# Row-tiled pairs for the maxima products of a two-layer attention kernel

## The reference

```python
def layer0(x, cond, attn_mask, ...):
    h = _ada_norm(x, cond, ln1_g, ln1_b, ada1_w, ada1_b)
    q, k, v = (_split_heads(h @ w + b) for w, b in ((wq, bq), (wk, bk), (wv, bv)))
    q, k = _apply_rotary(q, sin, cos), _apply_rotary(k, sin, cos)
    scores = einsum('bhqd,bhkd->bhqk', q, k) / sqrt(32)
    scores = where(attn_mask, scores, -inf)
    out = einsum('bhqk,bhkd->bhqd', softmax(scores), v)
    x = x + merge(out) @ wo + bo
    h = _ada_norm(x, cond, ln2_g, ln2_b, ada2_w, ada2_b)
    return x + gelu(h @ ff_w1 + ff_b1) @ ff_w2 + ff_b2

def layer1(x, c, ...):
    sh1, sc1, g1, sh2, sc2, g2 = split(silu(c) @ wc.T + bc, 6)
    x = x + g1 * gqa_attn(ln(x) * (1 + sc1) + sh1, wq, wk, wv, wo)   # 16 query heads, 4 key heads
    return x + g2 * (gelu((ln(x) * (1 + sc2) + sh2) @ w1.T + b1) @ w2.T + b2)
```

## Time and profile before

| what | before |
|---|---|
| median of 3 runs | 3960.23 us (3954.39 to 3964.08) |
| span of the profiled execution | 3966.3 us |
| PE busy | 3790.3 us (96%), 20404 products |
| DVE busy | 2467.7 us (62%) |
| ACT busy | 1601.7 us (40%) |
| POOL busy | 1603.3 us (40%) |
| mean granted clock of PE | 0.976 of full speed |

### The profile page before, as it was taken

How to read it: one execution, slowest core, us unless ns; L and a number is a source line. 1 busy time by engine, 2 the same in 40 slices (tenths; PEclk the granted TensorE clock), 3 DMA queues, 4 the chain that set the end, 5 groups by cost and what they waited for, 6 DMA issues and landing times.

```text
span 3966.3 us, 53519 instructions
## 1 busy us (share of the span) xinstructions
PE 3790.3 (96%) x20404; PEld 1507.3 (38%) x20404; DVE 2467.7 (62%) x3951; ACT 1601.7 (40%) x2807; POOL 1603.3 (40%) x907
## 2 busy tenths in 40 slices
PE   7988999999999999999999999999999999999999
PEld 4422444233443335432254323433244333533344
DVE  5687735766457655576654777367664776467752
ACT  1465313554125642155521663136521563126621
POOL 2466212673216632066510672136520672226611
PEclk8899999999999999999999999999999999999999
DMA  5233243212433123331233012311123112311122
GB/s 155 56 98 111 82 107 84 80 41 89 104 80 81 44 87 93 103 81 44 105 96 94 22 41 91 111 44 28 62 94 101 31 39 80 109 59 25 62 67 96
DMA packets 139021, 305.21 MB, mean 77 GB/s; under 512 B 19680, under 2 KB 59636, under 8 KB 137872
## 3 DMA queue, kind: packets, MB, share of 16 engines
q10 hardware_dynamic: 50944, 174.62, 13.6%
q1 hardware_dynamic: 87824, 127.17, 12.2%
HBM read 223.46 MB, written 36.66 MB: 66 GB/s over the span
## 4 chain that ended last, share of the span: by engine, by line
PE 83%; DVE 8%; POOL 3%; issue 3%; ACT 3%; DMA 1%; ACTq 0%; SPq 0%; POOLq 0%; DVEq 0%
PE ps L834 12%; PE ps L836 12%; PE ps L835 12%; PE ps L1014 11%; PE ps L935 9%; PE ps L997 8%; PE ps L871 7%; PE ps L1029 5%; DVE mcol L1517 3%; PE ps L888 3%; ACT probs L1194 2%; POOL sums L730 2%; DVE ring L1567 2%; PE ps L852 1%; DVE turn L1451 1%
## 5 line engine op out<-in xcount | busy, mean ns | idle before, releaser
L1517 DVE TENSOR_REDUCE mcol<-ps 128x1 f32<-128x512 f32 x2048 | 1288.5, 682 | 470.6 <-PE ps L935 470.2
L730 POOL TENSOR_TENSOR sums<-probs 128x1024 f32<-128x1024 f32 x448 | 1057.6, 2376 | 967.6 <-PE ps L1029 525.9
L1194 ACT ACTIVATE probs<-ps 128x512 f32<-128x512 f32 x2048 | 1098.2, 608 | 826.9 <-PE ps L997 592.8
L935 PE MATMUL ps<-ks,qs 97*128 97x512 f16 x2048 | 789.4, 389 | 61.3 <-DVE mcol L1517 43.6
L997 PE MATMUL ps<-qs,ks 98*128 98x512 f16 x2048 | 773.2, 387 | 72.3 <-ACT probs L1194 67.2
L1340 ACT ACTIVATE sums<-ps,cols 128x512 f32<-128x512 f32 x256 | 175.8, 687 | 1096.9 <-PE ps L836 1096.9
L1014 PE MATMUL ps<-probs,v_sb 128*32 128x512 f32 x4096 | 567.0, 628 | 0.0
L935 PEld LDWEIGHTS ps<-ks,qs 97*128 97x128 f16 x2048 | 201.2, 99 | 619.0 <-DVE mcol L1517 361.9
L834 PE MATMUL ps<-ring,probs 128*128 128x512 f16 x1024 | 388.0, 379 | 0.3 <-DVE probs L1612 0.3
L834 PE MATMUL ps<-aT,ring 128*128 128x512 f16 x1024 | 388.0, 379 | 0.0
L836 PE MATMUL ps<-aT,ring 128*128 128x512 f16 x1024 | 388.0, 379 | 0.0
(11 more groups left out here) (110 smaller groups left out, 3293.4 us busy)
## 6 DMA issues: line engine op xcount, KB each, us to landing
ring<-halves ACTq DMA_DIRECT2D x208, 512.0 KB, 3.4
qs<-hl SPq DMA_DIRECT2D x192, 128.0 KB, 4.0
ring<-halves SPq DMA_DIRECT2D x48, 512.0 KB, 6.3
ring<-in_weights ACTq DMA_DIRECT2D x39, 512.0 KB, 4.3
halves<-ring ACTq DMA_DIRECT2D x37, 512.0 KB, 2.9
ks<-hl SPq DMA_DIRECT2D x120, 128.0 KB, 4.3
dcopy<-inverses SPq DMA_DIRECT2D x56, 256.0 KB
probs<-in_x SPq DMA_DIRECT2D x8, 1024.0 KB, 8.3
```

Source lines behind the costliest of these rows:

```text
L730: pool.tensor_tensor(sums[:, m % SUM_SLOTS, :, :], prob(u - 2), prob(u), ALU.add).then_inc(sum_set[0].sem, 1)
L935: pe.matmul(bank, qs[0:K_MAX, hh, h, P * qt:P * qt + P], ks[0:K_MAX, key_set(i, hh), key_head(i, hh, h), 512 * half:512 * half + 512], sta ...
L1194: act.activation(prob(u)[:, e, :], ps[:, w % SCORE_BANKS, :], ACT.Exp).then_inc(exp_done.sem, 1)
L1517: dve.tensor_reduce(mcol[:, blk % 2, 4 * j + qt, half:half + 1], src, AX.X, ALU.max).then_inc(n_free[0], 1)
```

## The change

The stacks are laid out anew, so that the high x high rows of a head lie within the first 64 partitions for the even heads of a block and within the last 64 for the odd ones. In layer 0 the pair's rows are 0 to 32 and 64 to 96 (high part and mask row), in layer 1 0 to 63 and 64 to 96. In attention the maxima of two heads, over these rows alone, are issued as a pair (`max_pair`): two products over 33 (or 64) rows in different halves of the array, into two banks; the pair first waits for both banks. The products with low parts are thus left out of these maxima (in layer 1 the even heads keep one of the two); scores, from which they are subtracted, keep all rows. The 36 maxima outside attention stay products over 97 rows.

A step now issues one pair, then the four scores (with fills between the second and the fourth as before), then its other pairs. `MAX_AT_K` is made even, so that steps of block 1 in layer 0 have 4, 6, 4, 6, 4, 4 and 4 maxima in place of 5, 4, 5, 4, 5, 4 and 5.

SyncE's copies change with the layout: a layer 0 build is twelve DMAs of 64 partitions in place of six of 128, a layer 1 query build six in place of three, the row of maxima two in place of one, and the mask rows of layer 0 are two. The semaphore counts follow (`STACK_DONE`, `STACK_BEFORE`). The order of a block's heads in the packed weights and in the rotary table is changed to match.

```diff
@@ -25,7 +25,13 @@
-
+KEY_BASES = (((0, 65), (33,)), ((32, 64), (0,)))
+QUERY_BASES = (((0, 33), (65,)), ((0, 64), (32,)))
+PAIR_ROWS = (slice(0, HD + 1), slice(2 * HD, 3 * HD + 1))
+MASK_ROW, MAX_ROW = (HD, 3 * HD), 3 * HD + 1
+SHARED_KEY_BASES = ((0, 64), (32,))
+PLAIN_QUERY_BASES = (((0, 32), (64,)), ((32, 64), (0,)))
+PLAIN_PAIR_ROWS = (slice(0, 2 * HD), slice(2 * HD, 3 * HD + 1))
 NB = 2 * B
 UNITS, STEPS = 128, 64
...
@@ -38,7 +44,7 @@
 Q_CHUNKS = 2
 L0_CHUNKS, L1_CHUNKS = 24, 21
 MAX_AT = (4, 6, 8, 10, 12, 14, 16, 18, 20, 22, 24, 26, 28, 30, 32)
-MAX_AT_K = (0, 2, 5, 7, 9, 11, 14, 16, 18, 20, 23, 25, 27, 29, 32)
+MAX_AT_K = (0, 2, 4, 6, 10, 12, 14, 16, 20, 22, 24, 26, 28, 30, 32)
 WO_AT = 53
 LN2_AT = 60
 BIAS_AT = (49, 49, 50, 51, 53, 54, 56, 56)
...
@@ -66,7 +72,18 @@
 def max_tile(k):
-    return k // 2 % 4, k // 8, k % 2
+
+    pair, odd = divmod(k, 2)
+    return 2 * (pair // 8) + odd, pair % 8 // 2, pair % 2
+
+
+def slot_of(g, j):
+
+    return 4 * (j % 2) + 2 * g + j // 2
+
+
+def max_place(j, qt):
+    return 8 * (j % 2) + 4 * (j // 2) + qt
 def sum_of(u):
...
@@ -524,40 +540,52 @@
                 st, heads = key_set(i, hh), 8 if layer(i) == 0 else 4
                 if layer(i) == 0:
-                    m = mask_rows[i:i + 1, :].rearrange("o (h k) -> o h k", h=1).broadcast_to([1, heads, S])
+                    m = mask_rows[i:i + 1, :].rearrange("o (h k) -> o h k", h=1).broadcast_to([1, 4, S])
+                    for odd in range(2):
+                        r = MASK_ROW[odd]
+                        sp.dma_start(ks[r:r + 1, st, 4 * odd:4 * odd + 4, :], m).then_inc(mask_in[st], 16)
                 else:
                     m = ins["rows"][2:3, :].rearrange("o (h k) -> o h k", h=1).broadcast_to([1, heads, S])
-                sp.dma_start(ks[96:97, st, 0:heads, :], m).then_inc(mask_in[st], 16)
+                    sp.dma_start(ks[96:97, st, 0:heads, :], m).then_inc(mask_in[st], 16)
                 one = ins["rows"][1:2, :].rearrange("o (h k) -> o h k", h=1).broadcast_to([1, heads, S])
-                sp.dma_start(ks[97:98, st, 0:heads, :], one).then_inc(mask_in[st], 16)
+                sp.dma_start(ks[MAX_ROW:MAX_ROW + 1, st, 0:heads, :], one).then_inc(mask_in[st], 16)
             def put_stack(key):
                 kind, i, hh, th, part = key
                 done, _ = stack_done(key)
+                tok = slice(512 * th, 512 * th + 512)
                 if layer(i) == 0:
                     sp.wait_ge(st_lo, BUILDS[key] + 1)
-                    rows, heads, pieces = 16, slice(0, 8), [(0, 0), (0, 1), (1, 0), (1, 1)]
-                else:
-                    sp.wait_ge(*freed(key))
-                    sp.wait_ge(st_hi, BUILDS[key] + 1)
-                    rows, heads, pieces = 32, slice(4 * part, 4 * part + 4), [(0, BUILDS[key] % 2), (1, BUILDS[key] % 2)]
-                for low, x in pieces:
-                    src = hl[:, 2 * low + x, :]
-                    hi_at = (0, 64) if kind == "k" else (0, 32)
-                    for base in ((32 if kind == "k" else 64,) if low else hi_at):
-                        r0 = base + (16 * x if layer(i) == 0 else 0)
-                        if kind == "k":
-                            dst = ks[r0:r0 + rows, key_set(i, hh), heads, 512 * th:512 * th + 512]
-                        else:
-                            dst = qs[r0:r0 + rows, hh, heads, :]
-                        sp.dma_start(dst, src).then_inc(done, 16)
+                    for odd in range(2):
+                        half, slots = slice(64 * odd, 64 * odd + 64), slice(4 * odd, 4 * odd + 4)
+                        for low in range(2):
+                            for base in (KEY_BASES if kind == "k" else QUERY_BASES)[odd][low]:
+                                for x in range(2):
+                                    r = slice(base + ROT * x, base + ROT * x + ROT)
+                                    dst = ks[r, key_set(i, hh), slots, tok] if kind == "k" else qs[r, hh, slots, :]
+                                    sp.dma_start(dst, hl[half, 2 * low + x, :]).then_inc(done, 16)
+                    return
+                sp.wait_ge(*freed(key))
+                sp.wait_ge(st_hi, BUILDS[key] + 1)
+                for low in range(2):
+                    x = 2 * low + BUILDS[key] % 2
+                    if kind == "k":
+                        for base in SHARED_KEY_BASES[low]:
+                            sp.dma_start(ks[base:base + HD, key_set(i, hh), 0:4, tok], hl[:, x, :]).then_inc(done, 16)
+                        continue
+                    for odd in range(2):
+                        slots = slice(4 * odd + 2 * part, 4 * odd + 2 * part + 2)
+                        for base in PLAIN_QUERY_BASES[odd][low]:
+                            sp.dma_start(qs[base:base + HD, hh, slots, :], hl[64 * odd:64 * odd + 64, x, :]
+                                         ).then_inc(done, 16)
             def put_rows(i, blk):
                 hh, qc, g = block_of(blk)
                 sp.wait_ge(*freed(("rows", i, blk)))
-                d = qs[97:98, hh, 4 * g:4 * g + 4, :]
-                dst = bass.AP(d.tensor, d.offset, [[d.ap[0][0], 1], [P, 16], [1, P]])
-                sp.dma_start(dst, mT[:, :]).then_inc(max_in.sem, 16)
+                for odd in range(2):
+                    d = qs[MAX_ROW:MAX_ROW + 1, hh, 4 * odd + 2 * g:4 * odd + 2 * g + 2, :]
+                    dst = bass.AP(d.tensor, d.offset, [[d.ap[0][0], 1], [P, 8], [1, P]])
+                    sp.dma_start(dst, mT[8 * odd:8 * odd + 8, :]).then_inc(max_in.sem, 16)
             def totals_out(i, blk):
...
@@ -924,17 +954,32 @@
                                            start=(c == 0), stop=(c == C - 1))
                 mm.then_inc(n_full, 1)
+            def max_operands(key):
+                _, i, blk, k = key
+                hh, qc, g = block_of(blk)
+                j, qt, half = max_tile(k)
+                query = qs[:, hh, slot_of(g, j), P * qt:P * qt + P]
+                keys = ks[:, key_set(i, hh), key_slot(i, hh, g, j), 512 * half:512 * half + 512]
+                return j, query, keys
+
             def max_item(key):
                 _, i, blk, k = key
-                hh, qc, g = block_of(blk)
                 if k == 0:
                     stacks_ready(i, blk)
                 bank = bank_free(key)
-                j, qt, half = max_tile(k)
-                h = 4 * g + j
-                pe.matmul(bank, qs[0:K_MAX, hh, h, P * qt:P * qt + P],
-                          ks[0:K_MAX, key_set(i, hh), key_head(i, hh, h), 512 * half:512 * half + 512],
-                          start=True, stop=True).then_inc(n_full, 1)
+                _, query, keys = max_operands(key)
+                pe.matmul(bank, query[0:K_MAX], keys[0:K_MAX], start=True, stop=True).then_inc(n_full, 1)
+
+            def max_pair(two):
+
+                _, i, blk, k = two[0]
+                if k == 0:
+                    stacks_ready(i, blk)
+                banks = [bank_free(key) for key in two]
+                for bank, key in zip(banks, two):
+                    j, query, keys = max_operands(key)
+                    rows = (PAIR_ROWS if layer(i) == 0 else PLAIN_PAIR_ROWS)[j % 2]
+                    pe.matmul(bank, query[rows], keys[rows], start=True, stop=True).then_inc(n_full, 1)
             def stacks_ready(i, blk):
                 hh, qc, g = block_of(blk)
...
@@ -987,15 +1032,15 @@
             def score(i, w):
                 hh, qc, g = block_of(w // 32)
-                kt, h, bank = w % 32 // 4, 4 * g + w % 4, w % SCORE_BANKS
+                kt, j, bank = w % 32 // 4, w % 4, w % SCORE_BANKS
                 if w % 32 == 0:
                     pe.wait_ge(max_in.sem, max_in.at(i, w // 32 + 1))
                 if w >= SCORE_BANKS:
                     pe.wait_ge(exp_done.sem, exp_done.at(i, w - SCORE_BANKS + 1))
                 elif i >= 1:
                     pe.wait_ge(y_read.sem, y_read.at(i - 1, 5 + bank))
-                pe.matmul(ps[:, bank, :], ks[0:K_EXP, key_set(i, hh), key_head(i, hh, h), P * kt:P * kt + P],
-                          qs[0:K_EXP, hh, h, :], start=True, stop=True).then_inc(s_mm.sem, 1)
+                pe.matmul(ps[:, bank, :], ks[0:K_EXP, key_set(i, hh), key_slot(i, hh, g, j), P * kt:P * kt + P],
+                          qs[0:K_EXP, hh, slot_of(g, j), :], start=True, stop=True).then_inc(s_mm.sem, 1)
             def values(i, u):
                 hh, qc, g = block_of(u // 16)
...
@@ -1035,20 +1080,20 @@
                     u = 2 * s
                     if s < STEPS:
                         maxima, fills = maxima_at(i, s), FILLS[i].get(s, [])
-                        some(maxima[0:1])
+                        pairs = [maxima[n:n + 2] for n in range(0, len(maxima), 2)]
+                        for two in pairs[0:1]:
+                            max_pair(two)
                         score(i, 4 * s)
-                        some(maxima[1:2])
                         score(i, 4 * s + 1)
```

(17 more changed lines are left out.)

44 lines of the change are left out of this document (17 added, 27 removed).

## The result

The changed kernel takes 4074.88 us (median of 4 runs, 4070.29 to 4079.31) against 3959.94: a ratio of 1.0291, 95% interval 1.0276 to 1.0306, slower. Its profiled execution spans 4073.6 us, 107.3 more than the one before.

What follows compares the result with a forecast made beforehand. TensorE, busy for 96% of the span, was taken to bound the kernel. Terms 53 + 0 + 16 + 4 + 17 = +90 us on the 3960.2 median gave 4050 us; own range 4015 to 4095, wider range 3970 to 4160.

Steps and rivals of the forecast that it cites:

- a run of scores: In plain attention steps, score 3 waits for score 0's exponential, leaving TensorE idle 0.43 us, as much as the pairs save.
- The plain step: Attention step without projection or output tiles: 2.846 us becomes 0.175 us longer; 196 such steps in layer 1 give 34 us.
- Plain steps of layer 0: 158 attention steps, counted at two thirds because other engines hold part of them: 0.12 us each, 19 us.
- Projection steps: Attention steps with a projection: +0.39 us without totals, -0.25 with them, alternating; counted 0, with 10 us either way.
- SyncE's queue: Twelve DMAs instead of six delay layer 0's next block by 2 to 6 us: +16 us; second row DMA +4 us.
- TensorE's clock: Fewer products and more waits in layer 0 bring more 1.2 GHz stretches: a third more of 52 us, +17 us.
- A: Rival: row tiles in attention cost no mode change, plain step 2.833 us; 3993 us, chance 0.15.
- B: Rival: the halves of a pair run one after the other, plain step +0.593 us; 4175 us, chance 0.10.
- C: Rival: the clock falls in plain steps, a tenth more of attention at half rate, 98 us on top; 4148 us, chance 0.10.
- D: Rival: TensorE's saved time is passed on, projection steps giving 0.48 us each; faster, 3920 us, chance 0.10.

Runs made afterwards that it cites:

- e2: The changed kernel with two full 97-row products in place of each pair, order unchanged; 4075.72 us.
- e5: e2 with each two maxima products first waiting until both of their banks are free; 4092.28 us.
- e1: The changed kernel's new stacks and transfers, with the step order, maxima table and single products of the kernel before; 3971.62 us.
- e11: The changed kernel with single products between the scores in steps with a fill and the first three steps of layer 1 images; 4049.70 us.
- e4: The changed kernel with 19 further products, results overwritten, in the waits of the first three steps of each layer 1 image; 4069.11 us.
- e6: e1 with one pair in front of the scores in plain steps, except the first three steps of layer 1 images; 3970.38 us.
- e10: e6 with the query stack of layer 1 sent at step 17 instead of 20 and no pair in steps with totals; 3971.27 us.
- e7: e1 with the row of maxima ahead of the second key stack in layer 0's step 6, and query stacks at step 17 instead of 20; 4006.37 us.

## Why the prediction was right, and where its terms were not

It said slower and 4050 us; measured 4074.9, inside both ranges: +115 us where +90 was summed. The mechanism that it named first, a run of scores that waits for ScalarE in every plain step and takes what the pairs save, is what the runs show. That the sum came so near is in part luck: the 20 us of the queue hardly show in the changed kernel, while 16 and 21 us stand at two places that it counted as 0 and 2. By its own steps:

- **The plain step: right.** +0.175 us predicted, +0.194 measured. Every entry of the timetable stands in the trace: second half at 0.004 (0.007), score 0 at 0.32, score 3 at 1.40, second pair at 1.72 (1.705), values at 2.04 (2.02), next pair at 3.04 (3.02). The missing 0.02 lies within the changes of mode, at 0.10 instead of 0.093. Layer 1 gives 35.7 against 34. The Trainium skill (TensorEngine Tiling (Array Packing), Key Properties) says that a change of tiling mode drains TensorE; the trace agrees, at 0.10 us each.
- **Plain steps of layer 0: mis-sized.** 27.3 us against 19. In the 125 of them at full clock in both traces it is 11.9 us, 15.7 in the 33 others (27.6 by this second count). So the term itself was not too small; what it lacks is clock, which I had counted apart. The net sums of e2 (run +13.1, pairs +34) hide this: in steps at full clock in both traces e2, with the run and the new layout, costs 36 us more than before over layer 0, and it has 43 us less at 1.2 GHz.
- **Projection steps: mis-sized.** 0 predicted, +15.1 + 1.1 measured. The commonest step without totals takes 5.93 (5.83 predicted), one with totals 6.07 (6.05), so these two were right. The failing entry was that they alternate and cancel. They do in layer 1; but of the eleven such steps of a layer 0 image only three have totals (in image 1 they gain 2.4 us together), and eight have none and lose 5.6 together: the four that took 5.44 to 5.47 before lose 0.5, 0.5, 1.0 and 1.8. The number 5.93 has a part that I did not give it: with full products in the same order and no wait for both banks (e2) such a step already takes 5.74, with that wait (e5) 5.98. So with full products the order alone costs 0.30 and the second bank 0.24, where I gave the whole to the second bank.
- **SyncE's queue: the place right, the size wrong.** 16 + 4 predicted; e1 has 11, some of it in step 23 of layer 1 (step 20's extra issues, at which I counted nothing). In the changed kernel little of it shows at block 1 of layer 0: step 7 is longer by 1.0, 0.1, 0.1 and 1.6 us in the four images, against 1.0 to 1.9 in e1. The steps before it are longer, which gives the transfers time; in e11, where they are shorter again, it is 1.1 to 2.0.
- **TensorE's clock: mis-sized, and one place missed.** The +17 was a chosen third of the full-speed time lost in layer 0, 52 us. Counted so, as half of the time at 1.2 GHz, layer 0 goes from 55 to 85 us, +30, and layer 1 from 10 to 27, +17, where nothing was counted; these stand inside the sums by kind of step, not beside them. By the time at 1.2 GHz layer 0 has 59 us more and layer 1 has 34 more: 40 in the first steps, 6 fewer elsewhere. Those steps I had counted as plain, at 12 x 0.175 = 2 us; they lose 20.6. e4, e11 and e2 show that these are the run's waits and the lower clock behind them.
- **The rivals.** A fell with the 0.10 us of a change of mode, B with halves 4 ns apart. C's mechanism is seen in the starts of layer 1 and in layer 0, at less than its price of 98 us; plain steps of layer 1 hardly have it (1 us at 1.2 GHz in 184). D fell in e6 and e10 in its general form: TensorE's saved time isn't passed on. Its own price was high as well: it takes four products off a projection step (4 x 0.22) where two pairs save two.

What the prediction did not see is that the pairs come to nothing in sum: with full products in their places (e2) the time is the same. The new layout costs 11 of the 115 us (e1), and the order, the run of scores, the other 104 (e2 against e1). The pairs give 0.22 us in a plain step at full clock, in both layers, and the steps of layer 0 around its stretches at 1.2 GHz take that back and what layer 1 gained.

## What to carry to other kernels

Packing two products side by side saves their streaming time only if the order around them stays; price the changes of mode (here 0.10 us each and two more a step, against 0.44 us saved) and what the freed interleaving did: the products between the scores were what hid ScalarE's 1.08 us. Before an engine is relieved, look for steps in which it already waits, since there the gain turns into waiting. Sum by kind of step and look at the first steps of a stage apart: the same order that costs 0.19 us in the steady state cost 1.7 us a step there.

## What the runs showed of the hardware

- The two row tiles of a pair, 64 and 33 rows in different halves of the array, start 4 ns apart and end together. The Trainium skill (TensorE: Matmul & The Clock Gate, Part 3, The mechanism) has the same figure. The weight loads of a pair take 0.10 us together, as long as one took before.
- DMAs of half the size land sooner: `qs<-hl` of 64 KB 2.6 us after its issue where 128 KB took 4.0 before (medians). Each takes some 0.64 us of SyncE all the same (six of 128 KB in 3.85 us before, twelve of 64 KB in 7.64 in e7). Part of what the longer queue costs comes back so.
- Work that nothing needs can shorten a step: 19 further products in each image took 9 us off the starts of the four layer 1 images, in image 5 with the granted clock at 1.00 instead of 0.62 (e4).
